# Last stage of a gated attention and expert block: the turn and copy of the first norm, and the last pair's gating, in another order

## The reference

```
x = x + tanh(g_xattn) * cross_attention(layernorm(x), ctx, ctx)      # 16 heads of 8
y = layernorm(x)
a = self_attention(rope(y), causal)          # 16 heads of 8, in_proj weights
x1 = layer_norm(y + a @ out_proj.T + b) * ln1_w + ln1_b               # "first norm"
gates = softmax(x1 @ gate_w.T + gate_b)      # 8 experts
top2 of gates, all others zero
moe = sum over the two chosen experts of gate * (x1 @ expert_w[e].T + expert_b[e])
z = layer_norm(x1 + moe) * ln2_w + ln2_b                              # "second norm"
out = x + tanh(g_ffn) * z
```

## Time and profile before

| | us |
|---|---|
| median of three runs | 441.61 |
| profiled execution | 441.23 |
| its span | 439.4 |
| outside the span | 1.83 |
| step 4 to step 15, each | 6.60 |

### The profile page before, as it was taken

One profiled execution on the slowest core, in us unless ns is written; L12 is line 12 of the kernel. 1 busy time (PEld: TensorE's weight loads), 2 busy tenths in 40 slices (PEclk: granted clock), 3 DMA queues, 4 the chain that ended last, 5 costly groups with the idle time before them and its releaser, 6 DMA issues.

```text
span 439.4 us, 17671 instructions
## 1 busy us (share of the span) xinstructions
PE 385.7 (88%) x6538; PEld 231.3 (53%) x6538; DVE 369.2 (84%) x1188; ACT 288.4 (66%) x728; POOL 323.3 (74%) x740
## 2 busy tenths in 40 slices
PE   0368888888888899999999999999999999999994
PEld 0134544454444555666666666666655555555541
DVE  6587999999997878888878878877848999999987
ACT  1126777767766766666666666666665788788772
POOL 4456767767778988888888788849823788888884
PEclk9999999999999999999999999999999999999999
DMA  6855686685553333333434343333000000000001
GB/s 163 193 155 160 170 199 169 162 180 145 132 158 101 98 100 105 104 106 104 109 106 125 103 127 100 99 105 96 12 4 2 1 25 13 24 27 12 25 25 48
DMA packets 88037, 42.76 MB, mean 97 GB/s; under 512 B 16000, under 2 KB 87824, under 8 KB 87952
## 3 DMA queue, kind: packets, MB, share of 16 engines
q1 hardware_dynamic: 80864, 39.59, 34.2%
q10 hardware_dynamic: 7088, 2.04, 2.0%
HBM read 5.69 MB, written 2.10 MB: 18 GB/s over the span
## 4 chain that ended last, share of the span: by engine, by line
PE 41%; DVE 6%; ACT 5%; issue 3%; POOL 1%; SPq 1%; DMA 1%; POOLq 0%; ACTq 0%; DVEq 0%
PE s_bank L923 6%; PE u_bank L499 6%; PE st_bank L923 6%; PE s_bank L421 4%; PE s_bank L434 3%; DVE r L697 2%; PE t_bank L413 2%; PE u_bank L944 2%; PE u_bank L942 2%; PE u_bank L909 2%; PE t_bank L407 2%; ACT z_x_t L1018 2%; ACT part L577 1%; PE u_bank L514 1%; PE t_bank L408 1%
## 5 line engine op out<-in xcount | busy, mean ns | idle before, releaser
L716 DVE TENSOR_REDUCE nm<-s_bank 128x4 f32<-128x512 f32 x256 | 171.5, 683 | 36.3 <-PE s_bank L434 34.0
L599 ACT ACTIVATE pt<-st_bank 128x512 f32<-128x512 f32 x250 | 147.5, 602 | 74.0 <-PE st_bank L434 51.6
L434 PE MATMUL s_bank<-qk 64*64 64x128 bf16 (+1 forms) x1584 | 103.5, 220 | 12.1 <-DVE nm L716 5.7
L499 PE MATMUL u_bank<-pt,vaug 128*32 128x128 f32 x2048 | 108.3, 286 | 1.6 <-DVE ao L733 0.2
L434 PE MATMUL st_bank<-qk 64*64 64x128 bf16 (+1 forms) x1540 | 98.2, 218 | 0.0
L434 PEld LDWEIGHTS s_bank<-qk 64*64 64x64 bf16 (+1 forms) x1584 | 73.8, 104 | 36.1 <-issue 18.9
L434 PEld LDWEIGHTS st_bank<-qk 64*64 64x64 bf16 (+1 forms) x1540 | 69.1, 103 | 0.0
L499 PEld LDWEIGHTS u_bank<-pt,vaug 128*32 128x32 f32 x2048 | 41.1, 108 | 27.5 <-issue 5.2
L421 PE MATMUL s_bank<-mqk,idb 64*64 64x256 bf16 x256 | 38.3, 292 | 0.8 <-ACT pt L599 0.4
L327 POOL TENSOR_TENSOR part<-r,part 128x512 bf16<-128x512 f32 x32 | 37.1, 1158 | 1.4
L421 PE MATMUL st_bank<-mkq,idb 64*64 64x256 bf16 x244 | 35.7, 293 | 0.0
(11 more groups left out here) (136 smaller groups left out, 815.4 us busy)
## 6 DMA issues: line engine op xcount, KB each, us to landing
qk<-part SPq DMA_DIRECT2D x221, 128.0 KB, 2.8
x_all<-x SPq DMA_DIRECT2D x16, 128.0 KB, 2.6
qk<-qrow SPq DMA_DIRECT2D x32, 64.0 KB, 2.0
c_all<-ctx_in SPq DMA_DIRECT2D x14, 128.0 KB, 2.8
out<-z_o SPq DMA_DIRECT2D x14, 128.0 KB, 1.8
qk<-mts ACTq DMA_DIRECT2D x34, 32.0 KB, 2.7
qk<-mts SPq DMA_DIRECT2D x30, 32.0 KB, 2.1
ewt<-exp_t SPq DMA_DIRECT2D x1, 512.0 KB
```

What stands on the lines that cost most here:

```text
L434: ins = pe.matmul(to[outs, :], fixed[:, outs], moving, start=not masked, stop=True, skip_group_check=masked)
L499: ins = pe.matmul(u_bank[b][32 * j:32 * j + 32, r * P:(r + 1) * P], v, pt[m % 4][:, j, :], start=half == 0, stop=half == 1, skip_group_che ...
L599: act.activation(pt[m % 4][:, :, :].rearrange("k j q -> k (j q)"), transposed_bank(m)[:, :], ACT.Exp).then_inc(ex, 1)
L716: dve.tensor_reduce(nm[q % 2][:, first:first + HEADS], s_bank[n % 2][:, :].rearrange("q (j k) -> q j k", j=HEADS), AX_X, ALU.max, negate=T ...
```

## The change

Five things move; no instruction is added or taken away.

- TensorE: `gated_sum` is split. Its bias product (`sum_of_biases`) stays where it was, the first norm's turn follows it, and the sum product and the gates' turn come behind.
- ScalarE: `copy_x1(s-1)` goes from behind `copy_gates` to before `normalise2`.
- The step in which the last pair has its first norm (s = 16): TensorE turns the norm and the gates of pair 14 first, ScalarE copies both before the second norm, VectorE shifts the last pair's logits right behind its experts, and ScalarE takes the last pair's exponentials between the two halves of pair 14's gated copies.
- The step behind it (s = 17): VectorE does the last pair's gating before the paired sum of pair 14.
- The order of the remaining calls stays.

```diff
--- before.py
+++ after.py
@@ -931,7 +931,7 @@
                     pe.wait_ge(norm, SEQS - 1)
                 pe.transpose(u_bank[0][0:G * NE, W:W + P], zg[i][:, :, :].rearrange("q b e -> q (b e)"), idf[:, :]).then_inc(z_gt, 1)
 
-            def gated_sum(g, gc):
+            def sum_of_biases(g, gc):
                 i = gc % 2
                 pe.wait_ge(z_gtc, g + 1)
                 if gc == 0:
@@ -940,6 +940,9 @@
                     pe.wait_ge(z_all, (g - 1) * ALL + 1)
                 dst = u_bank[1][:, 0:W]
                 pe.matmul(dst, zgt[i][:, :], ebs[:, :], start=True, stop=False)
+
+            def gated_sum(g, gc):
+                dst = u_bank[1][:, 0:W]
                 pe.wait_ge(z_yq, g + 1)
                 pe.matmul(dst.rearrange("q (b d) -> q b d", b=G), idf[:, :], zyq[:, :, :],
                           start=False, stop=True).then_inc(z_yb, 1)
@@ -959,14 +962,21 @@
                     experts(s - 2, c - 2, 1)
                 if in_z(c, 0):
                     transpose_att(s, c)
+                if s - 1 == LAST:
+                    transpose_n(s - 1, c - 1)
+                    gates_t(s - 2, c - 2)
+                if in_z(c, 3) and s - 3 < LAST:
+                    sum_of_biases(s - 3, c - 3)
+                if in_z(c, 1) and s - 1 < LAST:
+                    transpose_n(s - 1, c - 1)
+                if s - 2 == LAST:
+                    gates_t(s - 2, c - 2)
                 if in_z(c, 3) and s - 3 < LAST:
                     gated_sum(s - 3, c - 3)
-                if in_z(c, 2):
+                if in_z(c, 2) and s - 2 < LAST - 1:
                     gates_t(s - 2, c - 2)
-                    if s - 2 == LAST:
-                        last_gated_sum(s - 2, c - 2)
-                if in_z(c, 1):
-                    transpose_n(s - 1, c - 1)
+                if s - 2 == LAST:
+                    last_gated_sum(s - 2, c - 2)
                 if in_z(c, 0):
                     project(s, c)
                 if in_z(c, 1):
@@ -1055,6 +1065,8 @@
                 if gc >= 1:
                     act.wait_ge(z_yp, g)
                 for b in range(G):
+                    if b == 1 and g == LAST - 1:
+                        gates_exp(LAST, gc + 1)
                     for e in range(HALF):
                         ins = act.activation(zyg[:, b, e, :], e_bank[b][1][:, e * P:(e + 1) * P], ACT.Copy,
                                              scale=zg[i][:, b, HALF + e:HALF + e + 1])
@@ -1072,22 +1084,25 @@
                     ins.then_inc(z_yg, 1)
 
             def body(s, c):
-                if in_z(c, 2):
+                if in_z(c, 2) and s - 2 < LAST:
                     gates_exp(s - 2, c - 2)
                 if in_z(c, 1):
                     normalise1(s - 1, c - 1)
                 if in_z(c, 0):
                     copy_att(s, c)
+                if in_z(c, 1):
+                    copy_x1(s - 1, c - 1)
+                if s - 1 == LAST:
+                    copy_gates(s - 2, c - 2)
                 if in_z(c, 4) and s - 4 < LAST - 1:
                     normalise2(s - 4, c - 4)
                 if s - 2 == LAST:
                     gate_last_experts(s - 2, c - 2)
-                if in_z(c, 2):
+                if in_z(c, 2) and s - 1 != LAST:
                     copy_gates(s - 2, c - 2)
-                if in_z(c, 1):
-                    copy_x1(s - 1, c - 1)
                 if in_z(c, 2) and s - 2 < LAST:
                     gate_experts(s - 2, c - 2)
+
             def early(n):
                 if n == DRAIN - 9:
                     copy_att(0, 0)
@@ -1260,14 +1275,19 @@
                                              in1=one(x_all, g * G + b), op0=ALU.mult, op1=ALU.add).then_inc(z_yo, 1)
 
             def body(s, c):
-                if in_z(c, 2):
+                if in_z(c, 2) and s - 2 < LAST:
                     shift_logits(s - 2, c - 2)
-                if in_z(c, 3) and s - 3 < LAST:
+                    if in_z(c, 3):
+                        gated_pairs(s - 3, c - 3)
+                    gating(s - 2, c - 2, (s - 3, c - 3) if in_z(c, 3) else None)
+                if s - 2 == LAST:
+                    gating(s - 2, c - 2)
                     gated_pairs(s - 3, c - 3)
-                if in_z(c, 2):
-                    gating(s - 2, c - 2, (s - 3, c - 3) if s - 3 < LAST else None)
+                    gated_sum(s - 3, c - 3)
                 if in_z(c, 2):
                     experts(s - 2, c - 2)
+                if s - 1 == LAST:
+                    shift_logits(s - 1, c - 1)
                 if in_z(c, 0):
                     attention_add(s, c)
                     experts_add(s - 3, c - 3)
```

## The result

The changed kernel takes 445.3 us (median of five runs, 445.11 to 445.89). The kernel before took 441.42 (five runs) in the same comparison, so the ratio is 1.009 with an interval of 1.0075 to 1.0105: slower by 3.9 us. The forecast was 444.6. The profiled execution took 445.26, with a span of 443.5 against 439.4 before.

The account below looks back on a forecast made before the run. Two circles of waits, both 6.60 us per step, were taken to bound the kernel. Steps 4 to 15 +3.7, step 3 0 and the tail -0.7 give +3.0 on the median of 441.61: 444.6 us, range 443.0 to 446.2.

Parts of the forecast that it names:

- the signs of both parts: Steps 4 to 15 slower by 3.7 us, steps 16 to 18 faster by 0.7 us.
- Circle B: Steps 4 to 15, norm's copy over logits and first expert product to the second: 6.60 before, forecast to shrink.
- Circle A: Steps 4 to 15, second expert product, norm's turn, its copy, gated copies, back: 6.60 before, forecast 6.91, +0.31 per step.
- the upper row: Bias product to sum product, 0.63, against 0.54 taken for the norm's turn; gave the upper bound of 0.40 per step.
- the lower rows: Step 16's second norm 0.79 and both copies 0.60, against 0.82 and 0.69; lower bound 0.19 per step.
- Slack: Steps 4 to 15: neither circle has slack to speak of, so a change helps only if it shortens both.
- Step 3: Has no second norm; its norm's turn must wait for the attention's copy; counted as 0, with -0.1 possible.
- keeps its distance: VectorE's paired sum moves with the next step's start at the same distance, so it adds nothing.
- The tail: Steps 16 to 18, last pair's logits and gating moved ahead: -0.7 us, bounds -1.0 and -0.2.
- Rival 1: Circle B alone counts, so faster: 438.2 us, at most 436; chance 0.08.
- Rival 2: The circles nearly balance, 12 x 0.06 is eaten by the tail: 441.6 us; chance 0.05.
- Rival 3: Slower by more, 0.40 per step and no gain in the tail: +4.8, 446.4 us; chance 0.07.

Follow-up runs that it names:

- the ScalarE part alone: Kernel before with only ScalarE's copy of the turned norm moved ahead of the second norm, TensorE and tail as before: 461.64 us, ratio 1.0464.
- the gates' copy first: Changed kernel with ScalarE copying the gates ahead of the second norm in all steps: 443.94 us, ratio 1.0067.
- the ninth copy: One extra gated copy (0.25 us of ScalarE) ahead of the eight: in the changed kernel 444.83 us, in the kernel before 444.07 us.
- the kernel with the steady steps alone: Changed kernel with both moved parts in the middle steps but the old tail: 447.71 us, ratio 1.0141.
- the kernel with the norm in halves: Gates-first kernel, first norm's bias folded into TensorE's bias product, second norm's two instructions in separate ScalarE gaps: 443.61 us, ratio 1.0049.

## Why the prediction was right, and where it was not

The forecast of slower by 3.0 was met with +3.9, inside the range, and the signs of both parts were right. But the mechanism of the steady steps was not the one forecast, so part of the hit is luck.

**The step that failed** is the sentence "Circle B doesn't pass through them", on the second norm and the copy of the gates. The logits' wait for the gates' copy was in the code. The kernel before could not show it as a wait, since that copy stood ahead of the norm's copy. So circle B is: turn at T+2.66, its copy 0.46 later, second norm 0.47, gates' copy 0.77, from its start to the logits 0.39, first expert product 0.44, second 1.80. That is 6.99, and the product started after 6.99. The expected "no idle before the logits" and "idle at the second expert product" came out the other way round. Shown by the ScalarE part alone (7.58 as this circle says), by the gates' copy first (the idle goes) and by the ninth copy (0.02 of its 0.25 shows).

**Circle A** was counted at 6.91 and is 6.77. Its terms were off in both directions: the turn came 0.64 behind the bias product, the upper row and not the chosen 0.54 (+0.10), as its weight load was not pulled ahead, against the rule on loads by which the prediction let the turn follow early; its copy came 0.46 behind it, not 0.42 (+0.04); second norm and gates' copy took 0.77 + 0.16 = 0.93 and not 1.04 (-0.11), near the lower rows; the gated copies 2.09 in place of 2.16 (-0.07); and the way from copies to product costs 0.16, not 0.26 (-0.10). In the gates-first kernel, where this circle binds, it is 6.86: there the gates' copy stands straight behind the norm's copy, must wait for its own turn, and starts 0.54 behind it.

**Slack**: the prediction said that neither circle has any. In the kernel before circle A had 0.10, by the ninth copy there. **The luck** is in the price per step, 0.31 by the wrong circle and 0.39 by the right one. They came close because both contain the second norm and the gates' copy, and in both the turn moves up first (0.73 forecast, 0.63 measured). Had circle A bound, its measured 6.77 would have made +0.17 per step, an estimate of +2.0 for twelve steps and +1.2 with the tail's -0.83, which is below the range.

**Step 3** at 0 was -0.07. **Step 4** held the one cost without a term, 0.56, from GpSimd's power beside the paired sum. The prediction said that VectorE's sum "keeps its distance"; it does so to TensorE, but in step 4 not to GpSimd. **The tail** at -0.7 measured -0.83, and -0.6 alone (medians; -0.76 by the spans). Its two halves were wrong and nearly cancelled: step 16 was to keep its length and lost 0.41, and the last gated copies were to follow the expert product, T+8.40 in all, but follow GpSimd's factors of the second norm, 2.42 behind that product's start in place of 1.92, T+8.49 in all. The range's lower end of 443.0 is also not what its own words give: 0.22 per step and a tail of -0.7 make 443.5.

**The rivals.** Rival 1 (circle B alone, faster) named the circle that does bind, and was wrong in its sign, for the same missing wait. The rule of the Trainium skill by which it stood (Perfetto Trace Analysis, Identifying the Most-Contended Engine, Optimization Strategy) would have the gaps of the most occupied engine found and what blocks them started sooner, though for TensorE it names other measures than the busy time used here. The change closed TensorE's 0.21 before the logits and opened 0.68 at the same place. Rival 2 fell with the step of 7.00. Rival 3 had the price per step right, 0.40, by the wrong circle, and the tail wrong.

## What to carry to other kernels

Before an instruction is moved on an in-order engine, list in the code every wait that its completion feeds, not only those that show as idle: a wait that is met early leaves no trace, and it becomes the bound when what it waits for moves back. Work out each circle of waits to its full length, and price the slack of each by one added instruction; two such kernels told more than any single timeline. And when a transfer of work off one circle brings nothing, look at when short operations on GpSimd start relative to VectorE's long ones.

## What the hardware showed beyond that

- **GpSimd's small operation stretches by its start.** The power on 128x2 takes 0.70 when it begins ahead of VectorE's paired sum, by as little as 0.03 (step 3 of the kernel before with a ninth copy), though the two then overlap. Begun 0.05 behind it takes 1.19, 0.18 behind 1.05 and 0.24 behind 1.01: it ends about 1.24 behind the sum's start each time, which is 0.55 behind the sum's end. Within 0.01 of the sum, in the kernel with the norm in halves, it took 1.25 six times and 0.70 three times. The sum reads two operands from SBUF. The Trainium skill (GPSIMD Engine Reference, Specifications) says that the two engines share SBUF interfaces and contend when VectorE reads two SBUF inputs; the trace agrees, and shows that here the order of the starts decides.
- **TensorE's clock.** With 1.22 idle per step the granted clock fell to 0.54 inside the long steps, which cost 1.6 to 2.1 each, while the steps between kept 1.00. In the kernel with the steady steps alone it fell to 0.56 once, after idle times of 0.52 and 0.68 in step 4. The changed kernel has the same 0.52 and 0.68 and kept its clock in all five executions (means of 0.996 to 0.998), so what decides is open.
- **A product that starts with its own load.** Behind idle time the expert product started at the same instant as its load, 0.05 after the release, and its first pass took 0.11 longer than one whose load had run ahead. And behind the bias product the next load was not pulled ahead, neither the sum product's into the same bank in the kernel before nor the turn's into another bank after it: 0.33 idle of the load both times, and 0.63 to 0.64 from product to product in place of 0.54.
